# Global attention: row maxima in units of 512 queries, and one list for TensorE over all groups

## What is computed

```python
q, k, v = (split_heads(x @ W + b) for ...)          # 16 heads of 8
att = einsum('bhqd,bhkd->bhqk', q, k) * scale
att = where(tril, att, -inf)
att = softmax(att, axis=-1)
y = einsum('bhqk,bhkd->bhqd', att, v)
```

## Time and profile before

| | us |
|---|---|
| median of three timed runs | 2748.99 (2748.05 to 2751.7) |
| profiled execution | 2754.7 |
| its span | 2752.8 |
| attention, from the first piece to the last output | 95 to 812 |
| exponentials, ScalarE busy | 311.1 |
| reductions of pieces, VectorE busy | 339.6 |

### The profile page before, as it was taken

One profiled execution on the slowest core, in us unless ns is written; L12 is line 12 of the kernel. 1 busy time (PEld: TensorE's weight loads), 2 busy tenths in 40 slices (PEclk: granted clock), 3 DMA queues, 4 the chain that ended last, 5 costly groups with the idle time before them and its releaser, 6 DMA issues. The chain is left out here.

```text
span 2752.8 us, 95843 instructions
## 1 busy us (share of the span) xinstructions
PE 2351.4 (85%) x36648; PEld 1451.3 (53%) x36648; DVE 2027.6 (74%) x2560; ACT 1707.2 (62%) x3577; POOL 911.8 (33%) x502
## 2 busy tenths in 40 slices
PE   2469868778873999999999999999998999999994
PEld 1113212122221667766766667666676667667674
DVE  5576636346216888888888888888888888888884
ACT  1005534434662777777776777677776777777773
POOL 4100000000002455454454544445444454444440
PEclk7559989899996999999999999999999999999996
DMA  3410020200000111211112111111112111211110
GB/s 101 60 38 1 10 29 1 28 11 1 3 1 8 33 30 31 53 48 29 31 38 57 35 31 30 51 47 30 29 41 58 32 29 30 53 45 34 30 30 24
DMA packets 63130, 89.59 MB, mean 33 GB/s; under 512 B 20050, under 2 KB 31072, under 8 KB 62640
## 3 DMA queue, kind: packets, MB, share of 16 engines
q1 hardware_dynamic: 62062, 81.89, 13.2%
q0 software_dynamic: 608, 1.37, 0.2%
HBM read 28.48 MB, written 4.39 MB: 12 GB/s over the span
## 5 line engine op out<-in xcount | busy, mean ns | idle before, releaser
L617 POOL TENSOR_TENSOR arena<-arena 128x1024 f32<-128x1024 f32 x192 | 466.8, 2431 | 1076.6 <-ACT arena L694 1076.6
L668 ACT ACTIVATE arena<-bank 128x512 f32<-128x512 f32 (+3 forms) x640 | 311.1, 551 | 455.4 <-PE bank L857 272.5
L1167 DVE TENSOR_REDUCE arena<-bank 128x1 f32<-128x1024 f32 (+7 forms) x384 | 339.6, 910 | 204.7 <-PE bank L836 140.8
L945 PEld LDWEIGHTS bank<-ident,arena 128*128 128x128 f32 x3072 | 341.5, 143 | 185.6 <-issue 115.2
L945 PE MATMUL bank<-ident,arena 128*128 128x128 f32 x3072 | 424.4, 281 | 13.1 <-DVE arena L1280 8.2
L719 ACT ACTIVATE arena<-bank 128x512 f32<-128x512 f32 x768 | 419.3, 604 | 25.0 <-PE bank L945 21.1
L939 PE MATMUL bank<-wqk,arena 128*128 128x512 f32 x768 | 390.3, 632 | 35.8 <-issue 22.0
L634 POOL TENSOR_TENSOR arena<-arena 128x1024 f32<-128x1024 f32 x96 | 182.4, 1900 | 631.2 <-ACT arena L694 631.2
L694 ACT ACTIVATE arena<-bank 128x1024 f32<-128x1024 f32 x192 | 196.4, 1023 | 311.0 <-PE bank L939 308.2
L1267 DVE TENSOR_REDUCE arena<-arena 128x16 f32<-128x1024 f32 x192 | 233.4, 1216 | 145.4 <-POOL arena L623 138.9
L833 PE MATMUL bank<-arena 128*128 (+4 forms) x640 | 212.4, 396 | 133.1 <-DMA arena<-in_c_zeros 86.6
(11 more groups left out here) (148 smaller groups left out, 3544.8 us busy)
## 6 DMA issues: line engine op xcount, KB each, us to landing
arena<-arena SPq DMA_DIRECT2D x768, 64.0 KB, 2.0
arena<-qk_parts SPq DMA_DIRECT2D x72, 128.0 KB
wqk<-in_L_ffn_Wqkv SPq DMA_DIRECT2D x12, 512.0 KB, 3.7
qk_parts<-arena SPq DMA_DIRECT2D x6, 512.0 KB, 2.6
wv<-in_L_ffn_Wqkv SPq DMA_DIRECT2D x6, 512.0 KB, 4.3
wo<-in_L_ffn_Wo SPq DMA_DIRECT2D x6, 512.0 KB, 4.0
w<-in_L_ffn_W SPq DMA_DIRECT2D x6, 341.0 KB, 3.0
out<-x SPq DMA_DIRECT2D x1, 1024.0 KB, 5.1
```

Of the source, the lines that this page charges most:

```text
L617: gp.tensor_tensor(rots[:, s], raw_qk[:, s], tab(l, t, s, 1).to_broadcast([P, H, DH]), ALU.mult).then_inc(done, 1)
L668: act.activation(ring[:, u % 8, lo:QC], bank[:, 4 + u % 3, lo:QC], ACT.Exp, scale=SCALE1).then_inc(exp_done, 1)
L945: last = pe.transpose(bank[:, out + b, P * (i % 4):P * (i % 4) + P], src[:, i].rearrange("p h d -> p (h d)"), ident[:, :])
L1167: ve.tensor_reduce(pmax[:, h * NT + t, c:c + 1], src, AX.X, ALU.max).then_inc(piece_read, 1)
```

## The change

Maxima are now made, turned and sent back in *units*: the four query tiles of one chunk for four heads, so a group has four units of 16 to 32 pieces, and 16 turns replace 4. A turn moves 16 rows. The first score of a chunk waits only for its own unit (`max_in`). The stack of group g is waited for ahead of its first piece. The list runs over all four groups: a scheduler takes the next item with the earliest start by the costs written in it (units of 10 ns), holds pieces back or pulls them ahead by `LEAD` (70 tiles a head ahead of the scores), and every engine's code is written out from it, without the loop. SyncE's part of the list begins behind the stacks, weights and biases as before.

```diff
+LEAD = 70
+def items_of(unit):
+    pieces = [("max", unit, h, t, c) for t in range(4 * unit, 4 * unit + 4) for h in range(HG) for c in range(1 + (t >= NT // 2))]
+    return pieces + [("turn", unit)]
 def schedule():
...
+    while score < HG * len(every) or part < len(items) or pv < len(every) or pending:
+        can = []
+        if score < HG * len(every):
+            k, qc, kt = every[score // HG]
+            if (k, qc) in unit_end:
+                at = max(unit_end[k, qc], exp_end[score - 3] if score >= 3 else 0)
+                can.append((max(at, clock["pe"]), 0 if clock["act"] < clock["pe"] + 60 else 3, "score"))
...
+            late = maxed < scored + HG * LEAD
+            can.append((max(at, clock["pe"]), (0 if late else 2) if clock["dve"] < clock["pe"] + 100 else 4, "part"))
+        begin, _, what = min(can, key=lambda c: (max(c[0], clock["pe"] + 8), c[1], c[2]))
+        if what == "score":
...
+            end = busy("pe", begin, 6 * width + 6)
...
+            exp_end.append(busy("act", end + 15, 10 + 13 * width))
...
+            if pv % len(steps) == 0:
+                stack_end[pv // len(steps) + 1] = pv_end[-1] + 400
...
+                part_end.append(busy("dve", busy("pe", begin, 6 * width + 8) + 10, 18 + 13 * width))
...
+                unit_end[k, unit] = part_end[-1] + 500
...
-            def maxima(g, slot):
-                sp.wait_ge(mpart_ready, g + 1)
...
+            def maxima(g, slot, u):
+                sp.wait_ge(mpart_ready, NQC * g + u + 1)
...
+            for k, what, *i in order:
+                if what == "turn":
+                    maxima(k, k % 2, i[0])
+                elif what == "pv" and i[0] == NS - 1 and k + 2 < NHG:
+                    sp.wait_ge(pv_done, NS * (k + 1))
+                    stack(k + 2, k % 2)
...
-                if (s, h) == (0, 0):
-                    pe.wait_ge(max_in, 16 * (k + 1))
+                if (kt, h) == (0, 0):
+                    pe.wait_ge(max_in, 16 * (NQC * k + qc + 1))
```

More of the change, by code:

```diff
@@ L137, in schedule, with busy @@
-    order += [("pv", len(steps) - 1), ("out", NQC - 1)]
-    return steps, pieces, order
+    every = [(k, *s) for k in range(NHG) for s in steps]
+    items = [(k, *i) for k in range(NHG) for u in range(NQC) for i in items_of(u)]
+    order, pending = [], []
+    clock = {"pe": 0, "act": 0, "dve": 0}
+    exp_end, part_end, pv_end, unit_end, stack_end = [], [], [], {}, {0: 0, 1: 200}
+    score, part, pv, scored, maxed = 0, 0, 0, 0, 0
+    def busy(engine, start, cost):
+        clock[engine] = max(clock[engine], start) + cost
+        return clock[engine]
@@ L141, in build @@
+    return steps, order
 def build(nc, a, out):
-    steps, pieces, order = schedule()
+    steps, order = schedule()
     NS = len(steps)
-    NPC = len(pieces)
+    index = {i: n for n, i in enumerate(i for u in range(NQC) for i in items_of(u))}
+    NPC = len(index)
     nc.disable_value_cache = True
@@ L669, in exps @@
                                        scale=SCALE1).then_inc(exp_done, 1)
-            exps(0)
-            with act.Fori(1, NHG) as k:
+            for k in range(NHG):
                 exps(k)
@@ L879, in turn_output @@
                 last.then_inc(oT_ready, 1)
[L881 to L896, removed]
             pe.wait_ge(identb_ready, 1)
@@ L901, in _ @@
             pe.wait_ge(ones_in, 16)
[L902 to L909, removed]
+            for k, what, *i in order:
+                if what == "score":
+                    scores(k, k % 2, *i)
+                elif what == "pv":
+                    values(k, i[0])
+                elif what == "out":
+                    turn_output(k, i[0])
+                elif what == "max":
+                    scores_for_max(k, k % 2, (what, *i))
+                elif what == "turn":
+                    turn_maxima(k, (what, *i))
             pe.wait_ge(oT_read, NHG * NQC)
@@ L1215, in _ @@
[L1215 to L1221, removed]
+            group_values(0)
+            for k, what, *i in order:
+                if what == "pv":
+                    qc, kt = steps[i[0]]
+                    if kt == QC // P * (qc + 1) - 1:
+                        ve.wait_ge(pv_done, NS * k + i[0] + 1)
+                        wait(ve, oT_ready, NQC * k + qc)
+                        ve.tensor_copy(o_sb, bank[:, 7, :]).then_inc(o_read, 1)
+                        if i[0] == NS - 1 and k + 1 < NHG:
+                            group_values(k + 1)
+                elif what == "out":
+                    qc = i[0]
+                    o = bank[:, 7, :].rearrange("p (t h d) -> p t h d", t=4, h=HG)
+                    r = rden.rearrange("p (t h o) -> p t h o", t=4, h=HG)
+                    ve.wait_ge(oT_ready, NQC * k + qc + 1)
+                    wait(ve, oT_read, NQC * k + qc)
+                    ve.reciprocal(r, o[:, :, :, D1:D1 + 1]).then_inc(den_ready, 1)
+                    ve.wait_ge(den_ready, NQC * k + qc + 1)
+                    dst = y[:, 4 * qc:4 * qc + 4, bass.ds(k, 1), :, :].rearrange("p t g h d -> p t (g h) d")
+                    ve.tensor_tensor(dst, o[:, :, :, 0:D1], r.to_broadcast([P, 4, HG, D1]), ALU.mult).then_inc(oT_read, 1)
+                elif what == "max":
+                    max_piece(k, (what, *i))
+                elif what == "turn":
+                    split_maxima(k, (what, *i))
```

165 lines of the change are left out of this document (83 added, 82 removed).

## The result

The changed kernel takes 2610.0 us (median of four runs, 2606.8 to 2611.4), the kernel before 2750.3 us beside it: 0.948 of the time (interval 0.947 to 0.950), 140 us less. The prediction said 2595 in a range of 2552 to 2646.

The account below looks back on a forecast made before the run. No engine is full throughout; the attention's microseconds come off one for one. 153 + 2 + 92 + 360 + 8 + 43 = 658 us for its end against 812.4, a gain of 154: median 2595 us, range 2552 to 2646.

Parts of the forecast that it names:

- Start: Up to the first score: SyncE's queue, with stack 1, weights and biases ahead of the first maxima transfer, sets 153 us.
- Phase A: First score to the turn of unit 3 of group 0: VectorE bounds it, 92 us (86 to 105), plus 2 for restart.
- round trips: Group 0, scores of units 1 and 2 due soon after their turns: waits of at most 1 us each.
- Phase B: From the turn of unit 3 of group 0 to the last turn: TensorE's 313 us packed at 0.87, 360 us.
- 8 us behind the stack: Groups 1 and 2: maxima transfers queue behind the stack's copies and stall TensorE, 8 us in all (0 to 16).
- Phase C: After the last turn, without pieces: 2.05 us a step for 18.25 full steps, 43 us in all (40 to 50).
- Registers: Old loop over groups 1 and 2: address registers, gone with unrolling, cause most of the 2 x 52 us over group 0.
- The stack's cover: Stacks 2 and 3 are wanted late enough to cover the 38 us copy; without it up to 18.5 us twice.
- the closer packing: Rival, chance 0.17: Phase B at 0.94, Phase A 86, Phase C 40, no queueing; attention ends at 612, kernel 2549 us.
- old group 0's pace: Rival, chance 0.17: Phase B at 0.82 (382), Phase A 105, Phase C 50, queueing 16; attention ends at 711, kernel 2648.
- the clock: Rival, chance 0.12: TensorE, partly used in Phase A, is granted only 0.62 there; +32 us, kernel 2626 us.

## Why the prediction was right

**Start, 153 us.** Measured 153.6. SyncE's list sets it, as the run that rearranges it shows with 41 us.

**Phase A, 92 + 2 us.** Measured 93.7. The size was right; the reason, VectorE as the bound, only in part: with half of each reduction left out it was 92.6 us from the first maxima transfer to the fourth instead of 99.9, 7 us less where 15 to 20 were expected. The prediction put the round trips at 1 us each. ScalarE's timeline of the changed kernel at unit 2's first score:

```profile
215.09 0.60 ACT L719 ACTIVATE arena<-bank 128x512 f32<-128x512 f32 x1 [13.99 <-remote]
```

The unit's turn comes at 207.59, so ScalarE first stands 6.5 us for pieces that VectorE has not reduced, and then 7.5 us for the turn and its round trip.

**Phase B, 360 us, and 8 us behind the stack.** Measured 374.6 us, of which 4.2 and 8.7 are the two stalls, so 361.7 us for the rest: a packing of 313/361.7 = 0.87, the value taken. The stalls, 12.9 us, were inside the bounds of 0 to 16. The out transfer took 23.7 and 31.5 us instead of 1.4, and holding the stack back took the wait away. The Trainium skill (*DMA: Bandwidth & Descriptors*, "Queues, rings and completion order") says that each DMA engine consumes descriptors in ring order; the traces agree. That 0.87 came out is luck in part, because its reasons did not hold. The prediction named as a sign of being wrong that VectorE idles over 20% of phase B: it was busy 283.79 of 375 us, so it idled 24%. With half of each reduction left out the packing rose only to 0.91, and costs taken from rows gave nothing (2616 us). What sets the 0.87 is left open; TensorE's busy time, 341 of 375 us, and the small effect of the rest point to its one in-order stream, but no run took work from TensorE.

**Phase C, 43 us.** Measured 52.5 us, the largest miss. The mis-sized term is the step, taken as 2.05 us and measured 2.54, slower even than the 2.45 of the earlier trace rows; over 18.25 steps that is 8.9 of the 9.5 us missed. The prediction set 0.97 us of exponentials against 0.98 us of value products and left out that the next score needs 0.43 us more until its exponential starts, and that the value product itself waits for the exponential just before it. The old order puts the value product behind all four scores; that this spares it the second wait is argued, and the run with the third score ahead (2.38 us a step) supports it.

**Registers.** Right: the unrolled kernel of before wins 55 us, and its groups 1 and 2 take group 0's time and the wait for the stack. The stack's cover was right too: no piece of the changed kernel waits for a stack. But without that cover the bill would have been 26 us twice, as in the unrolled kernel, and not up to 18.5.

**The sum.** 153.6 + 93.7 + 374.6 + 52.5 = 674.4 against 658, 16.4 us too few: 9.5 in phase C, 4.9 in the stalls, 1.7 in the rest of phase B, and 0.3 in the start and phase A together. The rivals: the closer packing didn't come, old group 0's pace (711) didn't either, and the clock was granted 0.89, 0.98 and 1.00 in the three stretches, so over a whole stretch it did not fall to the 0.62 of the first maxima. For 10 us of phase A it did, as the rival describes it: in the first of these stretches of the changed kernel TensorE made pieces at VectorE's pace and no scores. In phase B it fell behind the two stalls alone; the 8.71 us stall ends in the third stretch:

```profile
205.00:215.00 10.00, 5.62 (x18) 1.78 (x19) 8.49 (x16) 0.00 (x0) 0.00 (x0) 0.60 0.01 2
465.00:475.00 10.00, 5.36 (x51) 2.58 (x48) 4.83 (x5) 3.49 (x11) 0.00 (x0) 0.91 0.46 59
475.00:485.00 10.00, 5.72 (x27) 2.45 (x29) 3.96 (x5) 3.16 (x6) 0.00 (x0) 0.58 0.01 1
```

The stall is priced here by its wait alone; the slower products behind it are in the 361.7 us.

**Where the 140 us came from.** The start, 50 us (203.25 to 153.6). The loop written out, 53 us of attention by the run that does it alone. That leaves some 35 us, and no run isolates their cause. One candidate is the wait for the stack, 53 us in the unrolled kernel and none in the changed one. The run with late pieces removed it and won 7 us a group while crowding the pieces, which cost group 0 10 us; if it costs groups 1 and 2 as much, the wait is worth some 17 us in each, an estimate from these two figures, and that twice would be all of the 35. The other is that the maxima of one group may now stretch into the next, so that group 3's idle VectorE and TensorE are used; the run with LEAD at 50 shows that the distance matters (18 us for 20 tiles less). The 35 us are what is left with the two stalls, 12.9 us, paid.

## What to carry to other kernels

Before an engine's wait is priced, read the list of the queue that ends it: here a 12 KB transfer had been ready for some 40 us while SyncE waited for a copy that nobody needed yet, and moving blocks of issues at two places gave a further 60 us (2610 to 2550), 48 of them seen in the attention. A small transfer that is waited for must not be issued behind a large one that isn't; but tie the large one to a condition that can't drift, or it becomes the wait. When a loop's addresses lie in registers, price the unrolling apart from whatever comes with it.

## What the runs showed of the hardware

Value products of two heads, each head writing its own 32 partitions of the bank, took 0.97 us, those of four heads 0.98 us: four cost what two cost, so leaving two of the four out saved nothing. A transfer of maxima lands in 1.4 us without a stack ahead of it, and in up to 31.5 us behind 18 copies to eight partitions, although the DMA share is only 0.51 during these. And the layers behind, with the same instructions, took 1926 to 1947 us in traces of different kernels, a spread of 20 us and more than several effects that were looked for here.
